# Graph network on one core: the signals of the max pass given by a drain of TensorE

## The reference, cut to what matters

```python
msgs = z[edge_dst] @ Wd + z[edge_src] @ Ws + edge_weight[:, None] * ww[None, :] + bm
agg = jax.ops.segment_max(msgs, edge_dst, num_segments=n)
...
hidden = jax.nn.relu(z @ W1a + agg @ W1b + b1)
return hidden @ W2 + b2
```

## Time and profile before

| | us |
|---|---|
| median of 3 runs | 3882.38 (3880.49 to 3886.64) |
| span of the profiled execution | 3851.9 |
| around the span, median less span | 30.5 |

### The profile page before, as it was taken

How to read it: one execution, slowest core, us unless ns; L and a number is a source line. 1 busy time by engine, 2 the same in 40 slices (tenths; PEclk the granted TensorE clock), 3 DMA queues, 4 the chain that set the end, 5 groups by cost and what they waited for, 6 DMA issues and landing times.

```text
span 3851.9 us, 54329 instructions
## 1 busy us (share of the span) xinstructions
PE 3125.2 (81%) x21070; PEld 2150.6 (56%) x21070; DVE 1459.7 (38%) x3223; ACT 958.7 (25%) x2512; POOL 2340.9 (61%) x2327
## 2 busy tenths in 40 slices
PE   3788788878889888888857787878878787999898
PEld 2444444455557677777735555555656564555454
DVE  6555555223222111111224444544444443333333
ACT  2555455122222011010122222322222232000000
POOL 3666662666662665666446666666666662777775
PEclk7899999899999999999955665665665667999899
DMA  5444444655555666666433343433444337666564
GB/s 150 162 160 166 167 149 156 200 175 185 190 181 172 193 193 188 198 193 201 144 112 103 108 116 101 119 102 112 112 127 127 111 113 253 211 226 218 195 225 144
DMA packets 278767, 621.83 MB, mean 161 GB/s; under 512 B 60077, under 2 KB 188649, under 8 KB 270953
## 3 DMA queue, kind: packets, MB, share of 16 engines
q1 hardware_dynamic: 171944, 372.56, 28.5%
q0 software_dynamic: 104832, 244.47, 22.5%
q10 hardware_dynamic: 1728, 1.25, 0.1%
HBM read 477.62 MB, written 140.45 MB: 160 GB/s over the span
## 4 chain that ended last, share of the span: by engine, by line
PE 56%; another core or an unknown queue 15%; issue 13%; DVE 7%; ACT 6%; DMA 3%; SPq 1%; DVEq 0%; POOL 0%; ACTq 0%; POOLq 0%
PE banks L2056 27%; PE banks L1294 5%; PE banks L2077 4%; PE banks L554 3%; PE banks L2075 3%; PE banks L1283 3%; PE banks L1272 3%; PE banks L1274 1%; PE banks L529 1%; PE banks L2170 1%; PE banks L1154 1%; DMA ring_of_rows<-weight_parts 1%; ACT arena L2363 1%; ACT arena L1213 1%
## 5 line engine op out<-in xcount | busy, mean ns | idle before, releaser
L2056 PE MATMUL banks<-arena 128*128 128x384 bf16 (+1 forms) x9310 | 1557.1, 316 | 129.0 <-issue 114.3
L2056 PEld LDWEIGHTS banks<-arena 128*128 128x128 bf16 x9310 | 914.4, 100 | 618.0 <-issue 235.8
L516 POOL DMA_INDIRECT arena<-tab_l,ring_of_rows x831 | 808.4, 973 | 472.3 <-issue 286.3
L2121 POOL DMA_INDIRECT arena<-h_pieces,span_sources x450 | 435.8, 968 | 319.2 <-issue 108.3
L2121 POOL DMA_INDIRECT ring_of_rows<-message_pieces,span_sources x396 | 430.2, 1086 | 214.1 <-issue 98.0
L2121 POOL DMA_INDIRECT ring_of_rows<-x_pieces,span_sources x306 | 332.9, 1088 | 201.3 <-PE banks L2075 101.1
L1294 PE MATMUL banks<-arena 128*128 128x64 f32 x1662 | 349.8, 380 | 123.4 <-issue 123.0
L2101 DVE TENSOR_TENSOR arena<-iota_bf,span_targets 128x768 bf16<-128x768 bf16 x243 | 134.9, 556 | 822.3 <-remote 318.3
L2121 POOL DMA_INDIRECT ring_of_rows<-l_pieces,span_sources x306 | 300.7, 983 | 233.0 <-issue 71.8
L1294 PEld LDWEIGHTS banks<-arena 128*128 128x128 f32 x1662 | 315.9, 284 | 201.5 <-issue 190.4
L1388 DVE TENSOR_TENSOR_SCAN ring_of_rows<-arena,ring_of_rows,banks 128x512 f32<-128x512 bf16 x207 | 264.2, 1277 | 135.6 <-remote 57.7
(11 more groups left out here) (243 smaller groups left out, 3098.4 us busy)
## 6 DMA issues: line engine op xcount, KB each, us to landing
arena<-edge_counts SPq DMA_DIRECT2D x83, 896.0 KB
arena<-edge_counts SPq DMA_DIRECT2D x83, 672.0 KB
edge_counts<-arena SPq DMA_DIRECT2D x32, 1568.0 KB
typed_counts<-arena SPq DMA_DIRECT2D x27, 1568.0 KB
arena<-scan_mask SPq DMA_DIRECT2D x208, 128.0 KB
arena<-typed_counts SPq DMA_DIRECT2D x27, 896.0 KB
arena<-typed_counts SPq DMA_DIRECT2D x27, 672.0 KB
arena<-tab_l,ring_of_rows POOLq DMA_INDIRECT x831
```

The lines of the kernel that those rows point to most:

```text
L516: k.nc.gpsimd.indirect_dma_start(k.RG3[:, i % p.ring, at:at + width], None, table, bass.IndirectOffsetOnAxis(ap=k.SRC[:, i:i + 1], axis=0) ...
L2056: t = T.matmul(k.bank[i % N_SUMS][:, 0:rows.shape[-1]], counts[:, s, :], rows, start=s == 0 and n == 0, stop=s == NT - 1 and n == len(term ...
L2121: G.indirect_dma_start(k.rows[p.layer][s % n], None, k.pieces[p.layer], bass.IndirectOffsetOnAxis(ap=k.SRCG[:, at:at + 1], axis=0)).then_i ...
```

## The change

In four places the increment is taken off the last matmul and put on a `drain` instruction of TensorE that is issued right behind it. A drain lets TensorE's sequencer go on only once what was issued before it has finished; its increment follows. The matmuls, their order and every wait of every engine stay as they were, and no instruction of another engine is changed. In the order of instructions no row moves on any engine: a drain stands behind the last row of line 1154, 1274, 1283 and 1294 in each step. That makes 3 x 208 + 216 = 840 drains.

```diff
--- before.py
+++ after.py
@@ -1151,9 +1151,9 @@
         c = (4 * u + n) % QUARTER
         for h in range(2):
             at = slice(REC * h, REC * h + REC)
-            t = T.matmul(k.bank[typed_banks(i, u)[h]][:, n * KEYS:(n + 1) * KEYS], k.TSRC[quarter % 2][at, c, :],
-                         k.TKEY[quarter % 2][at, c, :], start=True, stop=True)
-    t.then_inc(k.sem("typed_counted"), 1)
+            T.matmul(k.bank[typed_banks(i, u)[h]][:, n * KEYS:(n + 1) * KEYS], k.TSRC[quarter % 2][at, c, :],
+                     k.TKEY[quarter % 2][at, c, :], start=True, stop=True)
+    T.drain().then_inc(k.sem("typed_counted"), 1)
 
 
 def vector_typed_one_hots(k, quarter):
@@ -1271,8 +1271,8 @@
             T.wait_ge(*p.landed(i))
             T.matmul(bank[:, q * P:(q + 1) * P], k.RG3[:, i % p.ring, UP:UP + H], k.IDENT, is_transpose=True, start=i == tiles[0], stop=False)
         T.wait_ge(k.sem(f"load_mask_{c % MASKS}"), 32 * (c // MASKS + 1))
-        T.matmul(bank[:, 0:len(tiles) * P], k.WW9, k.W9[c % MASKS][:, 0:len(tiles) * P], start=False,
-                 stop=True).then_inc(k.sem("l2_turned"), 1)
+        T.matmul(bank[:, 0:len(tiles) * P], k.WW9, k.W9[c % MASKS][:, 0:len(tiles) * P], start=False, stop=True)
+        T.drain().then_inc(k.sem("l2_turned"), 1)
 
     def turn_back(c):
 
@@ -1280,8 +1280,8 @@
         if c:
             T.wait_ge(k.sem("l2_back_copied"), c)
         for q in range(len(chunk_tiles(c))):
-            t = T.transpose(k.bank[BACK][:, q * P:(q + 1) * P], k.SCAN[c % 2][:, q * P:(q + 1) * P], k.IDENT)
-        t.then_inc(k.sem("l2_back"), 1)
+            T.transpose(k.bank[BACK][:, q * P:(q + 1) * P], k.SCAN[c % 2][:, q * P:(q + 1) * P], k.IDENT)
+        T.drain().then_inc(k.sem("l2_back"), 1)
 
     def select(c):
 
@@ -1291,8 +1291,8 @@
             T.wait_ge(k.sem("l2_selected"), c - 1)
         tiles = chunk_tiles(c)
         for q, i in enumerate(tiles):
-            t = T.matmul(window(k, c), k.RG3[:, i % p.ring, 0:H], k.HOT[:, c % HOT_RING, q, :], start=i == tiles[0], stop=i == tiles[-1])
-        t.then_inc(p.product, 1)
+            T.matmul(window(k, c), k.RG3[:, i % p.ring, 0:H], k.HOT[:, c % HOT_RING, q, :], start=i == tiles[0], stop=i == tiles[-1])
+        T.drain().then_inc(p.product, 1)
 
     turn_messages(0)
     turn_messages(1)
```

## The result

The change takes 4036.72 us (median of 4 runs, 4030.47 to 4042.44), the kernel before beside it 3882.05 us (4 runs, 3880.49 to 3886.64). The ratio is 1.0391, with a 95% interval of 1.0377 to 1.0406: 155 us slower, 0.74 us for each of 208 rounds. The profiled execution of the change has a span of 4038.2 us and took 4042.44 us.

The account below looks back on a forecast made before the run. In the max pass, TensorE's 4.72 us of work and its late signals were taken to make 5.94 us rounds. Tails 0.54 plus restart 0.40, over 208 rounds, gave 196; 3851.9 + 196 + 30.5 = 4078 us, range 3962 to 4194.

Parts of the forecast that it names:

- the favoured case: Max pass: drains wait as long as matmuls' signals do and add their own price; 4078 us (3962 to 4194), chance 0.50.
- the tails: TensorE's four steps a round in the max pass lose their overlap with the next step: 0.54 us a round.
- the restart: TensorE starting again after each drain in the max pass: 0.10 us a drain, 0.40 us a round.
- the hold: TensorE's signals in the max pass, late during GpSimd's gathers, stay as late with drains; nothing added or removed.
- the clock: TensorE's granted clock in the max pass; the favoured case had no term for it, 0 us a round.
- Drain held like the signal: The favoured case: a drain waits for held matmuls as their update does; 4078 us (3962 to 4194), chance 0.50.
- Nothing comes off: Max pass: drains take away none of the present waits, so their 196 us adds in full to 3851.9 us.
- Increment alone held: Rival: only a matmul's increment is late, a drain's is prompt; 3824 us (3687 to 3882), chance 0.30.
- The clock falls: Rival: signals prompt, but TensorE's clock drops toward 0.5; rounds of 6.3 to 6.7 us, near 4000 us, chance 0.11.
- Nothing changes: Rival: drains pass at once or lie in stands, signals as late as today; 3882 us within 10, chance 0.09.
- Around the span: Outside the profiled span: 30.5 us that the median shows, added to 4048 us to give 4078 us.
- GpSimd hidden: Max pass: GpSimd's gathers, 5.0 us a round, are hidden at 6.9 us a round and set nothing.

Follow-up runs that it names:

- e2: Kernel before with only the l2_back signal (behind line 1283) given by a drain, 208 drains; 3910.12 us, ratio 1.0083.
- e4: Kernel before with only l2_turned and typed_counted (lines 1154 and 1274) given by drains, 424 drains; 4035.11 us, ratio 1.0393.
- e1: Kernel before with the four increments left on the matmuls and a bare drain behind each; 4029.65 us, ratio 1.037.
- w6: Kernel before, no drains, TensorE waiting for its own four increments right behind each, in a group with late signals; 3973.6 us against 3845.8, ratio 1.0317.
- d2: Changed kernel with a second, bare drain behind each of the 840; 3681.28 us against 3362.5 for the kernel before, ratio 1.0936.
- w5: Kernel before, no drains, TensorE waiting for its own four increments, in a group without late signals; 3370.8 us against 3360.7, ratio 1.0029.
- a2: Changed kernel measured again, unaltered, in a group without late signals; 3539.46 us against 3360.7 for the kernel before, ratio 1.0524.
- h1: Kernel before with the max pass's gathers replaced by SyncE's plain loads of rows the edges don't name; 3178.01 us against 3362.5, ratio 0.9425.

## Why the prediction was right, and where not

**The size and sign** were right: 4078 us was forecast, 4036.72 came, within the favoured case's own range of 3962 to 4194. The pass ends at 3381.5 us (forecast near 3400), the round takes 6.67 us (forecast 6.9). The sum behind the number isn't what happened. Us a round:

| term | forecast | measured |
|---|---|---|
| the tails (lost overlap) | 0.54 | 0.36 |
| the restart (stands of 0.1 to 1 us) | 0.40 | 0.73 |
| the hold (stands over 1 us) | 0 | -0.74 |
| the clock (steps longer by themselves) | 0 | 0.35 |
| stands under 0.1 us | 0 | 0.03 |
| sum | 0.94 | 0.73 |

Three terms are off by 0.3 us or more and largely cancel, so the result is close partly by luck.

**Drain held like the signal.** The statement on the hardware is right, and shown by e2 and e4: a drain comes after all that is held before it. Its consequence for this kernel was wrong. The step that failed is "Nothing comes off": with four drains a round the hold mostly does not arise, 75 late drains of 840, and long stands fell from 228 to 75 us. I had taken the hold as given from outside. Both e1 and w6, which stop TensorE in two other ways, show the same: fewer late signals, also at an equal number of gathers. That it is the backlog of unfinished matmuls which does it fits all kernels but was not varied by itself, so it is an inference.

In "PSUM — Partial Sum Buffer" (Engine vs sequencer instructions) the Trainium skill says that "drain waits for the engine to go fully idle". The trace agrees: 2.2 us in e2 and 5.1 us in e4 after the matmuls' modelled ends.

**The tails** were taken too large, 0.54 for 0.36 us. Line 1283's tail of 0.21 us was worked out from its matmuls' spacing, but rows 5 have line 1154 start at 2506.10, 0.05 us before line 1283's end (0.07 us in the median of the pass). And the forecast added all four overlaps in every round, where some steps begin after a stand (122.6 us of stands before line 1294 in rows 3) and had none to lose.

**The restart** was mis-sized. I took 0.10 us a drain with an upper end of 0.15; from matmul to matmul it is 0.23 us (0.08 us in part of the rounds behind the turn back), and 0.17 for a drain by itself (d2). A wait on a semaphore was the wrong neighbour, as w5 shows, where TensorE goes on 0.06 us after the matmul's end: waiting is cheap, and the drain itself costs.

**Increment alone held (3824 us).** Its premise fell: e1's increments were on matmuls and came as in the change, and the drains of e2 to e4 were late by the microsecond. Its other half came true, that the "remote" waits vanish and consumers start within 0.06 us. It asked for a drain under 0.31 us, all told. Overlap and short stands come to 1.09 us a round, 0.27 a drain, which is under that limit; with the clock's 0.35 us it is 0.36, above it. The changed kernel without any hold (a2) confirms it: its round of 5.97 us is no shorter than the 5.92 of the kernel before with the hold.

**The clock falls (near 4000 us).** It did, from 0.61 to 0.55, not to 0.50 for good. This rival, given a chance of 0.11, described a part of the mechanism rather than another one: mostly prompt signals, slower work, 6.67 us a round where it gave 6.3 to 6.7. The favoured case had nothing for the clock, although half of the growth in TensorE's work is the clock's. The true account lies between the two.

**Nothing changes.** Excluded by 155 us.

**Around the span.** I added 30.5 us as what lies around the span. Every timed run shows its span about 4 us below its time (4038.2 and 4042.44). The rest of the 30.5 us is that the traced execution of the kernel before was faster than the timed ones. Against the traced spans the drains' 196 us met 186, against the medians 155.

**GpSimd hidden** held in the changed kernel. It would have been the key to the kernel without the hold, where GpSimd sets 5.15 us a round (w5) and the whole price of own waits hides behind it. There the drains cost 179 us, more than the 155 with the hold, which fits that they have no long stands to take away; the kernel before wasn't traced there.

## What to carry to other kernels

A signal showed no price of its own on the instruction that makes the result; a drain behind it costs TensorE the overlap of two steps (0.07 to 0.21 us here), up to 0.23 us of empty pipe, four times a round, and a slower clock (0.61 to 0.55). Where TensorE must be stopped behind a step, a wait for its own last increment was far cheaper than a drain (3 to 10 us against 179) where GpSimd set the pace and nothing was held; with the hold it cost 128 us against 155, in different groups. No run has it where TensorE sets the pace alone. And before a stall is taken as given, ask whether it depends on how far the stalled engine had run ahead: adding a stop may then shift the stall instead of adding to it.

## What the hardware showed that I had not expected

- **Two levels of one kernel.** 3885.2 and 3362.5 us on the same chip in two groups, 13.5% apart, with the hold in one and no late signal in the other. It differs in the other passes as well: the max pass starts near 1990 us with the hold and near 1700 without. Neither the chip nor the kernel decides it. What does stays open.
- **The hold follows the gathers.** In the whole kernel before, counting the signals of matmuls whose update can be put down to one matmul, of 258 with at most one gather issued in the 5 us ahead none was over 0.3 us late; with three it was 286 of 714 (mean 0.68 us over all), with four 397 of 565 (mean 2.65 us). Without the hold, four gathers delay none of 1468 (a2). So gathers are not enough for it, and no late signal was seen without them; a run with the hold and without gathers, which would show that they are needed, is missing.
- **Held matmuls pile up to a limit.** In the earlier passes TensorE stands with nothing to wait for (0.82 us in rows 8). When the signal at 1581.78 us came, at least 5.2 us late, 61 matmuls and weight loads had been started behind the latest matmul that it can belong to, and TensorE went on at 1581.79. Counted so, no signal in the whole trace came with more than 61 behind it. The Trainium skill gives a depth of 64 for TensorE's queue in "TensorE: Matmul & The Clock Gate" (Architectural detail); the trace agrees, within what can be counted.
- **A kernel without the lookup is 184 us faster than before (h1)**, with rounds of 4.32 us at a clock of 0.72 to 0.78, where GpSimd's gathers set 5.15 us in w5. No version found here beats the kernel before.
